# A two-layer graph network on one core: the first layer sums gathered rows of x in three bfloat16 parts instead of rows of x times w1

## The reference, cut to what matters

```python
# x: 6250 x 256 float32; 106250 edges (src, dst), sorted by the drawn dst, with self loops
def layer0(x, (dst_, src_), w0, w1):           # edge_index = stack([src, dst])
    messages   = (x @ w1)[src_]
    neighbours = segment_sum(messages, dst_, 6250)
    return relu(x @ w0 + neighbours)

x = layernorm(x + layer0(...))
x = layernorm(x + layer1(x, W, attn_src, attn_dst, edges, edge_type))   # 8 relations, 8 heads, softmax over edges
```

## Time and profile before

| | us |
|---|---|
| median of 3 runs | 2755.07 (2748.97 to 2756.56) |
| the profiled execution | 2753.87 |
| its span, first to last instruction | 2752.1 |
| sort | 0 to 250.4 |
| sum over gathered rows | 250.4 to 1427.0 |
| tail | 1427.0 to 1487.7 |
| layer two and last norm | 1487.7 to 2752 |

### The profile page before, as it was taken

The page is one execution under the profiler, slowest core; times in us unless marked ns, Lnnn a source line. Parts: engine busy times, 40 slices in busy tenths (PEclk is TensorE's granted clock), DMA queues, the critical chain, the costliest instruction groups (busy, mean ns, idle before and its releaser), DMA issues. The chain is left out here.

```text
span 2752.1 us, 38106 instructions
## 1 busy us (share of the span) xinstructions
PE 2301.1 (84%) x9936; PEld 1642.0 (60%) x9936; DVE 1938.4 (70%) x4273; ACT 1639.6 (60%) x3465; POOL 1846.5 (67%) x1875
## 2 busy tenths in 40 slices
PE   8697798999999999999997677787787777877775
PEld 3365566677777677777764555565555555655541
DVE  9896665555555555556553688888878887888887
ACT  4563554666666666666654566666666666666643
POOL 1002677777777777777753777777777777777745
PEclk9797899999999999999998789878978898888888
DMA  5202355754444444444454444554454445445535
GB/s 158 62 22 88 118 152 135 223 175 160 160 153 153 162 152 161 154 160 152 142 133 162 138 138 138 148 139 138 138 146 141 139 138 149 138 138 140 140 91 159
DMA packets 177777, 387.53 MB, mean 141 GB/s; under 512 B 42669, under 2 KB 106867, under 8 KB 171042
## 3 DMA queue, kind: packets, MB, share of 16 engines
q0 software_dynamic: 83888, 233.09, 30.1%
q1 hardware_dynamic: 86626, 99.05, 12.1%
q10 hardware_dynamic: 7056, 52.99, 5.0%
HBM read 302.96 MB, written 82.03 MB: 140 GB/s over the span
## 5 line engine op out<-in xcount | busy, mean ns | idle before, releaser
L1303 POOL DMA_INDIRECT region<-y_d,edge_z x856 | 877.6, 1025 | 468.8 <-issue 242.5
L1348 POOL DMA_INDIRECT region<-ha_d,idx_t x880 | 894.9, 1017 | 306.8 <-issue 237.4
L777 DVE TENSOR_TENSOR nodes<-ps,nodes 128x512 f32 x856 | 591.7, 691 | 507.0 <-PE ps L1687 383.4
L1687 PE MATMUL ps<-region 128*128 128x256 f32 x3424 | 798.2, 387 | 69.7 <-DMA region<-y_d,edge_z 40.3
L1687 PEld LDWEIGHTS ps<-region 128*128 128x128 f32 x3424 | 653.8, 193 | 232.6 <-issue 112.0
L1804 PE MATMUL ps<-region 128*128 128x264 f32 x1760 | 619.3, 481 | 164.2 <-DVE nodes L895 120.2
L1804 PEld LDWEIGHTS ps<-region 128*128 128x128 f32 x1760 | 345.0, 223 | 362.6 <-DVE nodes L895 241.3
L895 DVE TENSOR_TENSOR nodes<-ps,nodes 128x264 f32 x880 | 372.3, 423 | 54.2 <-DVE nodes L895 39.9
L1461 ACT ACTIVATE region<-iota_n,edge_z 128x256 f32<-128x256 f32 x856 | 364.8, 499 | 61.8 <-PE ps L1687 56.1
L1739 PE MATMUL ps<-region,edge_z 128*128 128x512 f32 x784 | 360.0, 592 | 5.7 <-ACT region L1503 4.5
L1503 ACT COPY region<-ps 128x512 f32<-128x512 f32 x196 | 114.7, 587 | 342.1 <-PE ps L1739 302.4
(11 more groups left out here) (265 smaller groups left out, 1857.2 us busy)
## 6 DMA issues: line engine op xcount, KB each, us to landing
ha_d<-region ACTq DMA_DIRECT2D x49, 1056.0 KB, 4.8
region<-near_d SPq DMA_DIRECT2D x55, 512.0 KB, 5.3
region<-ha_d,idx_t POOLq DMA_INDIRECT x880, 3.7
region<-y_d,edge_z POOLq DMA_INDIRECT x856
edge_z<-level_d SPq DMA_DIRECT2D x55, 136.0 KB, 4.0
kl_d<-region SPq DMA_DIRECT2D x8, 903.0 KB
edge_z<-kl_d SPq DMA_DIRECT2D x55, 129.0 KB, 2.2
y_d<-edge_z SPq DMA_DIRECT2D x25, 256.0 KB, 3.2
```

What stands on the lines that cost most here:

```text
L777: v.tensor_tensor(into, ps[:, u, :], into, ALU.add).then_inc(added0, 1)
L1303: g.indirect_dma_start(rows0[c % RING][:, u, :], None, y_d, bass.IndirectOffsetOnAxis(ap=y_idx[:, k:k + 1], axis=0), bounds_check=node_bou ...
L1348: g.indirect_dma_start(rows[s][:, k, :], None, ha_rows, bass.IndirectOffsetOnAxis(ap=idx_t[:, B * b + k:B * b + k + 1], axis=0), bounds_ch ...
L1687: mm = t.matmul(ps[:, u, h * D:(h + 1) * D], lhsT=sel0[c % SEL][:, u, h * P:(h + 1) * P], rhs=rows0[c % RING][:, u, :], start=True, stop=True)
```

## The change

- `y_d` and the product stage go. Instead each row of x is written to `x3_d` as three bfloat16 parts that add up to it. TensorE and ScalarE split them: ScalarE casts the row to bfloat16 (high, L1454), TensorE forms x - high in PSUM with an identity in float32 (L1707) and a negative identity in bfloat16 (L1709), ScalarE casts that (mid, L1459), TensorE forms x - high - mid in another bank (L1707, L1709, L1715), ScalarE casts that (low, L1464). x comes in 12 chunks of 4 x 128 rows and one of 106, each of two pieces of 512 columns, 25 pieces in all. Three banks rotate.
- Two pieces come between the counts and the transposes of v; the other 23 and the transpose of goes come before the transposes of q; none is in the loop. ScalarE clears `sums0` ahead of q's casts.
- The gathers fetch 1536 bytes a row. The one-hots are bfloat16, and `sum_columns` (L1792) makes three matmuls for each of the two halves of a column. What is summed is x, not x times w1.
- After the last column of a bucket TensorE transposes its sums (`turn_sums`, L1835), ScalarE copies them, and `node_products` (L1847, L1850) computes x w0 + sums w1 in PSUM with eight float32 matmuls. `sums0` is ordered by rank. Weights and columns of x are loaded for that.
- Offsets after `done_at`: sums + 1, products + 2, `node_sums` + 2, `inverse_deviation` + 5, turn + 4, units from + 5. The last two buckets have their own.
- The tile row shares memory with the bucket row and is loaded after the last column.

```diff
-            def products(tile):
-                it, h = tile // 2, tile % 2
-                if h == 0:
-                    t.wait_ge(xt_in[it % 2], 16 * (it // 2 + 1))
-                if tile >= 2:
-                    t.wait_ge(y_done, tile - 1)
-                for c in range(DC):
-                    mm = t.matmul(ps[:, tile % 2, :], lhsT=x_t[it % 2][:, c, h * P:(h + 1) * P], rhs=w01[:, c, :],
-                                  start=(c == 0), stop=(c == DC - 1))
-                mm.then_inc(y_ps, 1)
+        def piece_bank(j, low):
+            p = piece_of(j)[1]
+            return ps[p, (0, 1, 6)[(2 * j + low) % 3], 0:2 * D if j < 2 * WHOLE else D].rearrange("p (t n) -> p t n", n=D)
+        def bank_free(eng, j, low):
+            m = 2 * j + low - 3
+            if m >= 0 and m % 2 == 0:
+                eng.wait_ge(x_mid, m // 2 + 1)
+            elif m >= 0:
+                eng.wait_ge(x_low, m // 2 + 1)
...
+            def lift(j, low):
+                n, p, rows_at = piece_of(j)
+                bank_free(t, j, low)
...
+                t.matmul(piece_bank(j, low), lhsT=ident[p, p], rhs=x_in[n][p, rows_at, :], start=True, stop=False)
+                t.wait_ge(x_high, j // 2 + 1)
+                return t.matmul(piece_bank(j, low), lhsT=minus[p, p], rhs=x_parts[n][p, rows_at, 0, :],
+                                start=False, stop=not low)
+            def split_piece(j):
+                if j < PIECES:
+                    lift(j, 0).then_inc(x_rest, 1)
+                if j >= 1:
+                    lift(j - 1, 1)
+                    take_mid(j - 1)
...
             t.wait_ge(v_made, 1)
+            for j in range(FIRST):
+                split_piece(j)
             turn_rows(v_row, 4).then_inc(sort_ps, 1)
-            for tile in range(EARLY, Q_AT + 1):
-                products(tile)
...
+            for j in range(FIRST, PIECES + 1):
+                split_piece(j)
+            t.wait_ge(goes_made, 3)
+            t.transpose(ps[0:WW, 7, P:2 * P], goes_row, ident[:, :]).then_inc(sort_ps, 1)
...
+            for n in range(HELD):
+                a.wait_ge(x_stored[n], 16 * chunks_in(n))
+            a.wait_ge(setup, SU["minus_one"])
+            for n in range(4):
+                last = a.activation(sums0[:, n * NT * D // 4:(n + 1) * NT * D // 4], minus_one.to_broadcast([P, NT * D // 4]), ACT.Relu)
+            last.then_inc(sums_zero, 1)
...
                     for h in range(2):
-                        mm = t.matmul(ps[:, u, h * D:(h + 1) * D], lhsT=sel0[c % SEL][:, u, h * P:(h + 1) * P],
-                                      rhs=rows0[c % RING][:, u, :], start=True, stop=True)
+                        for k in range(PARTS):
+                            mm = t.matmul(ps[:, u, h * D:(h + 1) * D], lhsT=sel0[c % SEL][:, u, h * P:(h + 1) * P],
+                                          rhs=rows0[c % RING][:, u, k * D:(k + 1) * D], start=(k == 0), stop=(k == PARTS - 1))
                     mm.then_inc(segs0, 1)
...
+            def node_products(job):
+                par = job % 2
+                t.wait_ge(sums_turned, job + 1)
+                t.wait_ge(xt_in[par], 32 * (job // 2 + 1))
...
+                for h in range(2):
+                    for c in range(DC):
+                        t.matmul(ps[:, node_bank(job), h * D:(h + 1) * D], lhsT=x_t[par][:, c, h * P:(h + 1) * P],
+                                 rhs=w01[:, c, D:2 * D], start=(c == 0), stop=False)
+                    for c in range(DC):
+                        mm = t.matmul(ps[:, node_bank(job), h * D:(h + 1) * D], lhsT=sums_t[par][:, h, c, :],
+                                      rhs=w01[:, c, 0:D], start=False, stop=(c == DC - 1))
+                mm.then_inc(node_ps, 1)
...
                 for t in range(BK):
-                    if c == done_at(t) + 6:
+                    if c == done_at(t) + 5:
                         inverse_deviation(t)
```

More of the change, by code:

```diff
@@ L349, in graph_layers @@
         xt_in = [sem(f"xt_in{h}") for h in range(2)]
-        y_stored = [sem(f"y_stored{h}") for h in range(2)]
         x1_kept = [sem(f"x1_kept{h}") for h in range(2)]
@@ L808, in _ @@
             pad_rows()
-            v.wait_ge(jobs_made, 1)
-            job_regs = [v.alloc_register(f"sum_job{k}") for k in range(BK - 1)]
-            v.load(job_regs, job_row[0:1, 0:BK - 1])
-            jobs = [v.snap(r, min_val=0, max_val=BK - 2) for r in job_regs] + [BK - 1]
             for g in range(NG + LATE):
@@ L852, in _ @@
             v.wait_ge(begun, 1)
+            v.wait_ge(steps_stored, 32)
             v.wait_ge(acc_zero, 1)
@@ L1400, in _ @@
                              accum_out=cnt_all[:, t:t + 1]).then_inc(counted, 1)
-                keep_products(k + 1)
-            for tile in range(NPAIR - MASKED + 1, EARLY):
-                keep_products(tile)
+            round_high(0)
+            round_high(1)
+            for j in range(FIRST):
+                split_piece(j)
             a.wait_ge(sort_ps, PS["v"])
@@ L1664, in _ @@
                     settle(k - 1)
-                if y_tile_at(k) is not None:
-                    products(y_tile_at(k))
                 if k == 1:
```

275 lines of the change are left out of this document (183 added, 92 removed).

## The result

The changed kernel takes 2837.80 us, median of four runs (2826.34 to 2840.32), against 2755.82 us of the kernel before beside it (2748.97 to 2760.12, four runs). The ratio is 1.0289, 95% interval 1.0275 to 1.0304: 82 us longer, where the forecast was 22 us longer and its range ended at 2815. The profiled execution took 2840.32 us, its span 2838.5, so 86.4 us over the span before.

| from ... to | before, us | after, us | change | forecast |
|---|---|---|---|---|
| start to the first cast of q | 96.7 | 128.6 | +32.0 | +32.7 |
| to the first gather of the sum stage | 153.8 | 152.8 | -1.0 | -7.5 |
| to the end of the last gather (the stage) | 1176.6 | 1233.4 | +56.8 | +7 |
| to the first gather of layer two (the tail) | 60.7 | 60.0 | -0.7 | -10 |
| to the end | 1264.4 | 1263.7 | -0.7 | 0 |

The account below looks back on a forecast made before the run. GpSimd's gathers were taken to set the pace in the sum stage, VectorE's chain in the sort; +32.7 - 6.5 - 1 - 7 + 14 - 10 = +22 on 2753.9 gave 2776 us, range 2742 to 2815.

Parts of the forecast that it names:

- What bounds the kernel: GpSimd's gathers, one every 1.345 us, set the sum stage's pace; a faster TensorE gives back at most 14.4 us.
- Item 1: Sort: split at 3.38 us a piece, then store wait and clearing, delay q's casts to 129.3 us: +32.7 us.
- Rival A: Split's bank handover hides and the margin of 1.1 us holds: not slower, 2734 us; chance 0.13 in full, 0.22 half way.
- rival B: TensorE's clock falls in the split: at most 52 us more, 2828 us; chance 0.08.
- Item 2: Sort's loop: without nine tiles, two thirds of VectorE's waits go, -6.5 us; edges loading ahead of weights, -1.
- Item 3: Sum stage: larger rows cost GpSimd nothing, bfloat16 parts shorten TensorE's groups, half its lag's stalls go: -7 us.
- Rival D: Sum stage: weight loads beside each matmul make the parts useless, 5.2 us a group, about 450 us more; chance 0.01.
- Item 4: Sum stage: GpSimd's inverse deviation, one group earlier, waits for later statistics, 0.6 us a bucket: +14 us, bounds 0 and +69.
- margin of 1.1 us: Sum stage: statistics chain takes 14.8 us from the last gather, against 15.9 us of gathers in GpSimd's queue.
- rival C: Sum stage: stores and larger rows make landings 7.5 us, waits 3 us a bucket: 2831 us, half 2803; chance 0.09.
- Item 5: Tail, last gather to layer two's first: 60.7 us falls to 50, -10 us, bounds -5 and -14.
- The sum: Whole launch: +32.7 - 6.5 - 1 - 7 + 14 - 10 = +22 us, 2776 us.

Follow-up runs that it names:

- e13: Changed kernel with normalising, transposes and units at the places of the kernel before in 21 of 25 buckets, the last four closer step by step: 2773.88 us, ratio 1.0100.
- e2: Changed kernel with the clearing of the sums, and the wait for the stores of x's parts, moved from ahead of q's casts into the loop: 2812.13 us.
- e9: Changed kernel with the clearing moved into the loop and a fourth bank in the rotation of the split: 2796.32 us, ratio 1.0168.
- e1: Changed kernel with GpSimd's root, VectorE's normalising, TensorE's transposes and the units one group later in all but the last two buckets: 2835.33 us, ratio 1.0272.
- e3: Changed kernel with TensorE's node products of the bucket just completed ahead of the table unit of the bucket before: 2796.92 us, ratio 1.0138.
- e4: Changed kernel storing and gathering two of the three parts, 1024 B a row instead of 1536, the second part multiplied twice: 2834.23 us, ratio 1.0272.
- e7: Changed kernel with TensorE's transposes and units one group later in all but the last two buckets, GpSimd's and VectorE's order unchanged: 2797.42 us, ratio 1.0166.
- e14: Changed kernel with each table unit stored by itself, four stores of 264 KB instead of one of 1056 KB, attention columns first: 2790.94 us, ratio 1.0125.
- e8: Kernel before with VectorE normalising at done + 7 instead of done + 6, the group in which TensorE transposes the result: 2775.33 us, ratio 1.0087.
- e12: e11 with the last full bucket's transposes and node products ahead of the remaining units of the bucket before, behind the last sums: 2742.31 us, ratio 0.9981.
- spaced versions: Kernels built on the changed one with the spacing of e13, such as e13 itself, e11 and e12: 2773.88, 2744.61 and 2742.31 us.
- e11: Changed kernel with the spacing of e13, the clearing in the loop and a fourth bank in the split: 2744.61 us, ratio 0.9980.

## Why the prediction was wrong, by its own steps

**What bounds the kernel: right, and not carried far enough.** GpSimd's gathers set the pace before, and do again in e13. But the prediction worked out 42.7 us of TensorE against 47.9 and called the rest "10% of air". TensorE's work was 45.3 (a group 2.69 us instead of 2.62, and 3.8 behind each wait, with the clock at 0.96 over the stretch), and the air was then 2 us. An engine's in-order waits belong into the same sum as its work; I asked that only of GpSimd.

**Item 1, the split and the clearing, +32.7: right.** Measured +32.0, with the piece at 3.31 us, clock 1.00, stores landed at 117.6, clearing 11.1. e2 and e9 confirm both halves: 17.9 us were the clearing and the stores ahead of q, 15.2 the bank's handover. That TensorE waits for a bank with nothing to do between was the reading of the order, and a fourth bank removed just that. Rival A (q cast before 110) and rival B (pieces of 5.7 us) are both out.

**Item 2, the loop, -6.5 and -1: the term did not come.** Measured -1.0. The prediction laid VectorE's 9.9 us of waits for the settle to the nine tiles. Without the tiles the wait is still there (VectorE, 98 to 281 us, changed kernel; then e2):

```profile
DVE region L670 <- PE ps L1764: 9.2, 7, 2.2
...
DVE region L670 <- PE ps L1768: 3.7, 4, 1.7
```

It scatters by itself. Seven kernels have the changed loop as it stands (changed, e1, e3, e4, e7, e13, e14), and it took 146.9 to 152.8 us; the three long ones (changed, e3, e13) have 13.3 to 14.5 us of VectorE's waits for TensorE at a clock of 0.74 to 0.75, the four short ones 9.0 to 9.4 us at 0.76 to 0.77. The loop of the kernel before took 153.8, and 151.4 in e8, whose sort is the same. So the nine tiles brought anything from -1 to 7 us, and one profile can't tell. My term had a precision that wasn't there.

**Item 3, the parts and the larger rows, -7: right in kind.** GpSimd's waits for sums, 30.0 us before, are 22.7 in all; behind the 0.3 us of issue the real stalls fell from 14.4 to 9.2, so -5. e4 shows the bytes at nothing that can be told. Rival D is refuted: 24 matmuls took 2.69 us.

**Item 4, the new wait, +14: the step that failed.** Measured: 66 us. The margin of 1.1 us was computed for one chain on an idle TensorE: it starts 4.6 us behind the gather's issue, the landing alone, where TensorE in fact started 10.9 us behind it in the bucket above, on rows that had landed after 5.5. What the prediction didn't list is who else waits where the jobs move together: it followed the root's move and overlooked that VectorE's normalising and TensorE's transposes now stand in the same group, with four to eight additions between, and that VectorE itself now waits for TensorE's node products ahead of them. All of it can be read in the code: normalise at done + 6 and transposes at done + 7 before, both at done + 4 after. The size agrees with rival C (3 us in most buckets, 2831), its stated cause doesn't: landings were 3.6 us in the median and not 7.5, e4 took a third of the bytes away, and e1 gave every chain 5.3 us more, and the waits stayed. That C's number comes near is luck. e7, e8 and e13 put in its place: TensorE's wait of 4.0 us a bucket, with the slower group behind it, fills TensorE's time, 50.2 us a bucket against 47.1 of gathers; 3.1 us times 24 buckets is 74 us; the changed stage is 65 us longer than that of e13. What share the 1056 KB stores have in it is open, since e14 changed the order of the units with them.

**Item 5, the tail, -10: wrong.** Measured -0.7. By the terms: from the end of the last gather to the end of its sum 13.3 us where 7.6 to 10 were taken. TensorE had three groups still to sum when the gathers ended, and ahead of the last it waited 1.6 us more for the last landing, which came 10.5 us behind the gather's end (11.5 behind its issue); 5 were taken. The kernel before had 16.8 us from that end to its node sums, and the prediction gave no reason why that should halve. Then 5.2 us of three units of the bucket before, not in the sum at all; transposes to turned rows 10.4 against 8.7; units 24.8 against 22.4. These are the rows (GpSimd, TensorE, GpSimd):

```profile
1513.79 1.02 POOL L1373 DMA_INDIRECT region<-x_d,edge_z  x1 [0.30 <-issue]
...
1525.38 2.86 PE L1792 MATMUL ps<-region 128*128 128x256 bf16 x24 [1.61 <-DMA region<-x_d,edge_z]
1528.08 5.32 PE L1874 MATMUL ps<-region,edge_z 128*128 128x512 f32 x12
1533.23 0.60 PE L1835 MATMUL ps<-ident,nodes 128*128 128x128 f32 x4
...
1544.95 5.42 PE L1874 MATMUL ps<-region,edge_z 128*128 128x512 f32 x12 [0.67 <-ACT edge_z L1588]
...
1574.81 1.09 POOL L1418 DMA_INDIRECT region<-ha_d,idx_t  x1 [28.09 <-PEq L1910]
```

Moving the three units (e12) brought nothing. The tail of e14 is 2 us shorter, in one profile. Why the tails of the spaced versions (62.4 to 70.1 us) are longer than that of the changed kernel is shown only in part, by the rows of e11; it stays open, and with it what the tail could come down to.

**The sum.** Of the 64 us between forecast and result, 50 are item 4 with item 3, 9 the tail, 6 the loop, -1 the way to q.

## What to carry to other kernels

When a change moves jobs closer to each other in a table of places, write down for each pair of engines that hand over, in which group each stands before and after; two that stood one group apart and now stand in the same one are a wait of the second for everything that the first has queued in that group. Add such waits to the engine's work before comparing it with the bound: an engine with 10% of air can lose all of it to one of them. And where a wait shows up on the pace-setting engine, give it a group more: if it stays, it is lateness and not latency, and its cause is on the other engine.

## What the runs showed of the hardware

- A gather instruction of 128 rows costs GpSimd the same at 1024 B and 1536 B a row, 1.018 and 1.015 us in the median, and the waits for the statistics behind it didn't move either (42.7 against 42.1 us in the stretch).
- The median gather of the changed kernel landed 3.6 us behind its issue, of those whose landing the profile has. The last four of the changed kernel took 10.8 to 11.9 us, while the mean busy share of the DMA engines was 1.00 from 1510 to 1515 us and 1.02 from 1515 to 1520; loads of x had been issued from 1504 to 1509.
- Behind a wait of TensorE of 3.41 us the granted clock was 0.50 from 1108 to 1110 us and 1.00 again from 1112, and the group of 24 matmuls in between took 3.8 us instead of 2.69.
- The store of 1056 KB landed in 4.9 us in the median, that of 264 KB in 3.3. The page DMA: Bandwidth & Descriptors of the Trainium skill, section Anatomy of one DMA, gives 2.0 us plus the bytes over 436 GB/s, a fit for transfers that GpSimd issues; these stores are issued by ScalarE. By it they would take 4.5 and 2.6 us, an estimate. The difference between the two is near (1.9 by the fit, 1.6 measured), the fixed part is larger here.
- A stretch of matmuls that lifted the granted clock from 0.50 to 1.00 ahead of the loop left the clock from 110 to 240 us at 0.79 and the loop's length within 1 us.
- The same loop code took 146.9 us in one launch (e4) and 152.8 in another (changed kernel), with mean granted clocks of 0.77 and 0.74 in it and 9.4 and 14.5 us of VectorE's waits for TensorE; which is cause and which effect wasn't tried.
